# Attention slots joined in pairs on every engine of a two-layer transformer kernel

## The chip, the cores and the metric

The kernel runs on one core of one Trainium2 chip. The metric is the device time of one execution in microseconds. The core has TensorE (PE; its weight loads are shown as PEld), VectorE (DVE), ScalarE (ACT), GpSimd (POOL) and SyncE (SP, which here issues DMAs). Each runs its own instructions in the order in which they are written; they meet at semaphores.

## The reference

x is [8, 512, 256] in float32 (8 batch entries, 512 tokens, width 256). Four layers follow each other, each on the normalized x and added to x: a gated mixer over a context, a feed-forward layer, cross-attention, and a feed-forward layer with 8 experts. The change touches only the cross-attention, which is (cut to what matters):

```python
def _L1_xattn_ref(query, key, value, ...):        # query: layernorm(x); key, value: context
    q = (query @ W_Query + B_Query).reshape(B, Lq, 16, 64)
    k = (key @ W_Key + B_Key).reshape(B, Lk, 16, 64)
    v = (value @ W_Value + B_Value).reshape(B, Lk, 16, 64)
    scores = jnp.einsum('bqhd,bkhd->bhqk', q, k) / D ** 0.5
    probs = jax.nn.softmax(scores, axis=-1)
    out = jnp.einsum('bhqk,bkhd->bqhd', probs, v)
    return out.reshape(B, Lq, 1024) @ W_Output + B_Output
```

## The kernel before

`attention` works on 64 units, one after the other: a unit u is one pair of heads (2 x 64 = 128 rows) of one batch entry, `U = HP * B` with 8 pairs and 8 entries. In a unit there are `NBL` = 8 tiles j: 2 heads by 4 blocks of 128 queries. A tile has 128 x 512 scores. Its way is:

- TensorE, `score` (L905): two matmuls into one of two banks of PSUM (`S_BANK + j % 2`). The operands are of type fp32r. Keys and queries are split into a high and a low part for that. `score` may write a bank when the exponential of tile j - 2 has read it (semaphore `exp`).
- VectorE, `row_max` (L1040): the negated maximum of each row.
- ScalarE (L997): the exponential into one of four tiles `Pr`, and the row's sum.
- VectorE, `row_sum` (L1045): the reciprocal of the sum. GpSimd (L1018): multiplies the tile by it.
- TensorE, `turn` (L916): four transposes of 128 x 128 into one of two banks (`T_BANK`). VectorE, `keep` (L1052), copies them to `PT`; for tiles 4 and 5 ScalarE does it (L1010).

Once per unit there is more. `project` (L884) makes the queries (k = 0) and keys (k = 1) of unit u + 1, `project_values` (L893) its values, `weigh_values` (L926) multiplies the turned tiles of unit u - 1 with its values, and `output` (L936) applies the output weights in two halves, which VectorE's `add_out` (L1059) adds to x. The queries and keys of u + 1 are split: ScalarE's `queries` (L966) and `keys` (L973) write the high part, VectorE's `queries` (L1027) and `keys` (L1034) the low part. The keys are then copied by four DMAs from `k_own` to `k2`, which holds each head's keys twice (L867); SyncE issues them when both parts of the keys are there:

```python
                for u in range(U):
                    sp.wait_ge(s["kh"], u + 1)
                    sp.wait_ge(s["kl"], u + 1)
```

and the first score of the unit waits for their landing:

```python
                    if j == 0:
                        pe.wait_ge(s["ql"], u + 1)
                        pe.wait_ge(s["k2"], 64 * (u + 1))
```

The order is written out by hand on each engine, as a loop over u (65 turns, since the end of a unit's work falls into the next) and over the slots j = 0 to 7. TensorE's slot is `score(u, j)`, then `turn(u, j - 2)`, then the extra work: a projection of unit u + 1 in slots 0 and 1, the weighing of u - 1 in slot 2, the values of u + 1 in slot 4, the outputs of u - 1 in slots 5 and 6. VectorE's slot is `row_sum(u, j - 1)`, `row_max(u, j)`, `keep(u, j - 2)`; its `queries` come in slot 1, its `keys` in slot 2, `add_out` in slot 7. ScalarE's slot is one exponential, with `queries` in slot 0, `keys` in slot 1, `heads_out` (L983, the weighed values of u - 1) in slot 4 and `values` (L978) in slot 5.

Of the kernel before, what the change touches and what calls it, by code (L numbers as in the profile page):

```python
# [17 lines left out]
ACT = mybir.ActivationFunctionType  # L18
# [3 lines left out]
P = 128  # L22
B, S, D = 8, 512, 256
N = B * S
TPB = S // P
# [327 lines left out]
def wait_count(eng, sem, value):  # L353

    if value > 0:
        eng.wait_ge(sem, value)
# [457 lines left out]
def attention(nc, c, x_all, xnT_all, ctxT_all, first, Wq, Wk, Wv, Wo):  # L814
# [3 lines left out]
    with ExitStack() as ctx:  # L818
# [28 lines left out]
        def there(u):  # L847
            return 0 <= u < U
# [6 lines left out]
        with nc.Block() as block:  # L855
# [15 lines left out]
            def _(pe):  # L871
# [37 lines left out]
                def turn(u, j):  # L909
                    pe.wait_ge(s["pn"], NBL * u + j + 1)  # L910
                    if j >= 2:
                        wait_turned_copies(pe, u, j - 1)
                    elif u:
                        wait_turned_copies(pe, u - 1, NBL - 1 + j)
                    for t in range(TPB):
                        ins = pe.transpose(ps[:, T_BANK + j % 2, P * t:P * t + P], Pr[:, j % 4, P * t:P * t + P],  # L916
                                           c["ident"][:, :])
                    ins.then_inc(s["t_ps"], 1)
# [22 lines left out]
                project(0, 1)  # L941
                project_values(0)
                for u in range(U + 1):
                    for j in range(NBL):
                        if there(u):
                            score(u, j)
                            if j >= 2:
                                turn(u, j - 2)
                        if j < 2 and there(u - 1):
                            turn(u - 1, NBL - 2 + j)  # L950
                        if j < 2 and there(u + 1):
                            project(u + 1, j)
                        if j == 2 and there(u - 1):
                            weigh_values(u - 1)
                        if j == 4 and there(u + 1):
                            project_values(u + 1)
                        if j in (5, 6) and there(u - 1):
                            output(u - 1, j - 5)

            @block.scalar  # L960
            def _(act):
                def queries(u):
                    act.wait_ge(s["q_ps"], u + 1)
                    for h in range(2):
                        own = slice(AD * h, AD * h + AD)
                        ins = act.activation(q2[own, u % 2, h, :], ps[own, A_BANK, :], ACT.Identity,  # L966
                                             bias=b_s[own, 0, u % HP:u % HP + 1])
                    ins.then_inc(s["qh"], 1)

                def keys(u):  # L970
                    act.wait_ge(s["k_ps"], u + 1)
                    wait_count(act, s["k2"], 64 * u)
                    act.activation(k_own[:, 0, :], ps[:, A_BANK + 1, :], ACT.Identity,  # L973
                                   bias=b_s[:, 1, u % HP:u % HP + 1]).then_inc(s["kh"], 1)

                def values(u):
                    act.wait_ge(s["v_ps"], u + 1)
                    act.copy(V[:, u % 2, :, :], ps[:, A_BANK, :].rearrange("p (t d) -> p t d", t=TPB)  # L978
                             ).then_inc(s["V"], 1)

                def heads_out(u):
                    act.wait_ge(s["pv"], u + 1)
                    act.activation(oT[:, :], ps[:, O_BANK, :], ACT.Identity, bias=b_s[:, 2, u % HP:u % HP + 1]  # L983
                                   ).then_inc(s["oT"], 1)

                act.wait_ge(s["scaled"], 1)
                queries(0)
                keys(0)
                values(0)
                for u in range(U + 1):  # L990
                    for j in range(NBL):
                        if j == 4 and there(u - 1):
                            heads_out(u - 1)
                        if there(u):
                            act.wait_ge(s["nmax"], NBL * u + j + 1)
                            wait_count(act, s["t_ps"], NBL * u + j - 3)
                            act.activation(Pr[:, j % 4, :], ps[:, S_BANK + j % 2, :], ACT.Exp,  # L997
                                           bias=nmax[:, j % 4:j % 4 + 1], accum_out=rsum[:, j % 4:j % 4 + 1]
                                           ).then_inc(s["exp"], 1)
                        if there(u + 1):  # L1000
                            if j == 0:
                                queries(u + 1)
                            if j == 1:
                                keys(u + 1)
                            if j == 5:
                                values(u + 1)
                        if there(u) and j - 2 in ON_ACT:
                            act.wait_ge(s["t_ps"], NBL * u + j - 1)
                            q = P * ((j - 2) % TPB)
                            act.copy(PT[:, u % 2, (j - 2) // TPB, :, q:q + P],  # L1010
                                     ps[:, T_BANK + j % 2, :].rearrange("p (t q) -> p t q", t=TPB)
                                     ).then_inc(s["pt_a"], 1)

            @block.gpsimd
            def _(pool):
# [6 lines left out]
            def _(dve):  # L1022
# [20 lines left out]
                def row_sum(u, j):  # L1043
                    dve.wait_ge(s["exp"], NBL * u + j + 1)
                    dve.reciprocal(rinv[:, j % 4:j % 4 + 1], rsum[:, j % 4:j % 4 + 1]).then_inc(s["rinv"], 1)  # L1045
# [9 lines left out]
                def add_out(u, half):  # L1055
# [12 lines left out]
                dve.wait_ge(s["w"], 16 * 3)  # L1068
                dve.tensor_scalar(w_rest[:, 0, :, :], w_rest[:, 0, :, :], AD ** -0.5, None, ALU.mult
                                  ).then_inc(s["scaled"], 1)  # L1070
                for u in range(U + 1):
                    for j in range(NBL):
                        if there(u):
                            if j >= 1:
                                row_sum(u, j - 1)
                            row_max(u, j)
                            if j >= 2:
                                keep(u, j - 2)
                        if j < 2 and there(u - 1):
                            keep(u - 1, NBL - 2 + j)  # L1080
                        if there(u + 1):
                            if j == 1:
                                queries(u + 1)
                            if j == 2:
                                keys(u + 1)
                        if j == 7:
                            if there(u):
                                row_sum(u, j)
                            if there(u - 1):
                                if u > 1:  # L1090
                                    dve.wait_ge(s["x"], 2 * (u - 1))
                                add_out(u - 1, 0)
                                add_out(u - 1, 1)


def load_expert_weights(sp, ew, w1, w2):
# [643 lines left out]
```

## Time and profile before

| | |
|---|---|
| Time, median of 3 runs | 1924.83 us (1918.81 to 1925.09) |
| Profiled execution, its own time | 1923.95 us |
| Its span, first to last instruction | 1922.2 us |
| Mean granted clock of TensorE, share of full | 0.925 |
| Busy: TensorE, weight loads, VectorE, ScalarE, GpSimd | 1711.2, 1162.7, 1205.1, 844.4, 645.5 us |
| First and last start of a score (L905) | 471.2 and 1630.3 us |
| Scores' matmuls, transposes (counts) | 1024 and 2048 |
| DMAs of the keys (L867) | 256 of 256 KB |

The profile is that of one execution. Times in it count from the first instruction. TensorE's matmuls overlap and their ends are modelled, so the starts of neighbouring instructions tell the pace, not the durations. "Idle before" is how long an engine stood still before an instruction, and what ended that. The attention stage is the longest stage of the program and lies between 471 and 1645 us.

### The profile page before, as it was taken

Reading aid. Unit: us, or ns where it says so; the run is one execution under the profiler, and the core shown is the slowest. Engines: PE = TensorE matmul, PEld = TensorE weight load, DVE = VectorE, ACT = ScalarE, POOL = GpSimd, SP = SyncE. Lnnn points to the kernel's source line nnn. Section 1 sums busy time; section 2 is a strip of 40 time slices with the busy share of each in tenths; the row PEclk is TensorE's granted clock in tenths of the full one; section 3 lists DMA queues with packets and bytes.
Section 4 is the critical chain, followed back from the end, with each engine's and each line's share of the span. In section 5 each row is a group of like instructions: output and inputs, shape, how many; then the busy total and the mean of one; then the engine's idle time right before and its main releaser. Section 6 shows DMA issues by size and latency. Waiting matters only on the chain. (4 is left out here: it accounts for less than half of the span.)

```text
span 1922.2 us, 26211 instructions
## 1 busy us (share of the span) xinstructions
PE 1711.2 (89%) x8900; PEld 1162.7 (60%) x8900; DVE 1205.1 (63%) x2743; ACT 844.4 (44%) x1870; POOL 645.5 (34%) x745
## 2 busy tenths in 40 slices
PE   6569999996999999999999999999999999742564
PEld 4456777764666666666666666666666666631343
DVE  5444444432777777777777777777777776657731
ACT  3224433332555555555555555555555555110111
POOL 2154444430333323323323333333333233100885
PEclk9669999998999999999999999999999999555777
DMA  7100000003221222222322222212212221250244
GB/s 249 20 22 12 12 12 1 1 0 102 66 66 45 67 64 46 66 59 52 67 53 58 67 49 62 67 44 67 66 45 66 62 49 45 92 176 0 48 73 58
DMA packets 66658, 109.47 MB, mean 57 GB/s; under 512 B 16088, under 2 KB 48096, under 8 KB 66528
## 3 DMA queue, kind: packets, MB, share of 16 engines
q1 hardware_dynamic: 60384, 99.29, 20.9%
q0 software_dynamic: 6144, 8.52, 2.9%
q8 instruction: 72, 1.18, 0.3%
q14 instruction: 58, 0.48, 0.1%
HBM read 27.84 MB, written 12.85 MB: 21 GB/s over the span
## 5 line engine op out<-in xcount | busy, mean ns | idle before, releaser
L1018 POOL TENSOR_SCALAR at_Pr<-at_Pr,at_rinv 128x512 f32<-128x512 f32 x512 | 355.8, 695 | 824.3 <-DVE at_rinv L1045 824.3
L997 ACT ACTIVATE at_Pr<-at_ps,at_nmax 128x512 f32<-128x512 f32 x512 | 352.0, 687 | 522.4 <-DVE at_nmax L1040 520.8
L1040 DVE TENSOR_REDUCE at_nmax<-at_ps 128x1 f32<-128x512 f32 x512 | 351.1, 686 | 138.2 <-PE at_ps L905 127.3
L905 PE MATMUL at_ps<-at_k,at_q 128*128 128x512 f32 x1024 | 420.6, 492 | 9.4 <-DMA at_k<-at_k_own 7.7
L916 PE MATMUL at_ps<-k_ident,at_Pr 128*128 128x128 f32 x2048 | 310.7, 274 | 4.4 <-POOL at_Pr L1018 4.4
L916 PEld LDWEIGHTS at_ps<-k_ident,at_Pr 128*128 128x128 f32 x2048 | 249.3, 140 | 94.1 <-POOL at_Pr L1018 33.2
L1052 DVE COPY at_PT<-at_ps 128x512 f32<-128x512 f32 x384 | 261.5, 681 | 0.0
L905 PEld LDWEIGHTS at_ps<-at_k,at_q 128*128 128x128 f32 x1024 | 174.4, 190 | 129.0 <-issue 119.5
L926 PE MATMUL at_ps<-at_PT,at_V 128*64 128x512 f32 x1024 | 235.5, 602 | 0.9 <-DVE at_PT L1052 0.9
L1045 DVE RECIPROCAL at_rinv<-at_rsum 128x1 f32<-128x1 f32 x512 | 83.4, 163 | 174.9 <-ACT at_Pr L997 173.0
L926 PEld LDWEIGHTS at_ps<-at_PT,at_V 128*64 128x64 f32 x1024 | 68.2, 137 | 122.6 <-issue 121.5
L936 PE MATMUL at_ps<-at_wo,at_oT 128*128 128x256 f32 x512 | 131.6, 380 | 0.8 <-ACT at_oT L983 0.8
L446 PE MATMUL mm_ps<-mx_w,mm_hT 128*128 128x256 f32 x512 | 120.9, 382 | 0.0
L436 PE MATMUL mm_ps<-m_xnT,mx_w 128*128 128x512 f32 x256 | 111.2, 592 | 1.3 <-ACT m_xnT L589 1.3
L893 PE MATMUL at_ps<-at_w_rest,m_ctxT 128*128 128x128 f32 x896 | 109.2, 275 | 0.0
L884 PE MATMUL at_ps<-m_xnT,at_w_rest 128*128 128x512 f32 x224 | 106.8, 599 | 0.0
L884 PE MATMUL at_ps<-m_ctxT,at_w_rest 128*128 128x512 f32 x224 | 105.4, 593 | 0.0
L893 PEld LDWEIGHTS at_ps<-at_w_rest,m_ctxT 128*128 128x128 f32 x896 | 104.5, 192 | 0.0
L446 PEld LDWEIGHTS mm_ps<-mx_w,mm_hT 128*128 128x128 f32 x512 | 93.7, 190 | 16.6 <-issue 5.3
L1027 DVE SCALAR_TENSOR_TENSOR at_q<-at_ps,m_b_all,at_q 64x512 fp32r<-64x512 f32 x128 | 96.0, 750 | 8.3 <-ACT at_q L966 5.4
L997 ACT ACTIVATION_READ_ACCUMULATOR at_Pr<-at_ps,at_nmax 128x1 f32 x512 | 98.6, 193 | 0.0
L936 PEld LDWEIGHTS at_ps<-at_wo,at_oT 128*128 128x128 f32 x512 | 87.4, 190 | 8.3 <-ACT at_oT L983 1.7
(251 smaller groups left out, 2099.1 us busy)
## 6 DMA issues: line engine op xcount, KB each, us to landing
at_k<-at_k_own SPq DMA_DIRECT2D x256, 256.0 KB, 4.2
k_x<-in_x SPq DMA_DIRECT2D x8, 512.0 KB, 7.8
mg_ctx<-in_ctx SPq DMA_DIRECT2D x8, 512.0 KB, 7.9
mx_ctxn<-in_ctx SPq DMA_DIRECT2D x8, 512.0 KB, 3.8
rows<-lo_xn SPq DMA_DIRECT2D x8, 512.0 KB, 3.0
r_w<-in_L_ffn_w SPq DMA_DIRECT2D x16, 256.0 KB, 5.3
out<-k_x SPq DMA_DIRECT2D x1, 4096.0 KB, 16.9
mx_w<-in_L_ffn_w SPq DMA_DIRECT2D x2, 1024.0 KB, 10.3
```

Source lines behind the costliest of these rows:

```text
L436: ins = pe.matmul(ps[:, H_BANK + f % 4, :], w1_s[:, k, P * f:P * f + P], xnT_all[:, k, b * S:b * S + S], start=k == 0, stop=k == DC - 1)
L446: ins = pe.matmul(ps[:, Y_BANK + t // 2, D * (t % 2):D * (t % 2) + D], hT[:, f, P * t:P * t + P], w2_s[:, f, :], start=f == 0, stop=f == F ...
L884: ins = pe.matmul(ps[:, A_BANK + k, :], weights(k, d, hp), src[:, d, b * S:b * S + S], start=d == 0, stop=d == DC - 1)
L893: ins = pe.matmul(ps[:, A_BANK, P * t:P * t + P], ctxT_all[:, d, b * S + P * t:b * S + P * t + P], weights(2, d, hp), start=d == 0, stop=d ...
L905: ins = pe.matmul(ps[:, S_BANK + j % 2, :], q2[:, u % 2, h, q:q + P], k2[:, u % 2, h, part, :], start=part == 0, stop=part == 1)
L916: ins = pe.transpose(ps[:, T_BANK + j % 2, P * t:P * t + P], Pr[:, j % 4, P * t:P * t + P], c["ident"][:, :])
L926: ins = pe.matmul(ps[AD * h:AD * h + AD, O_BANK, :], V[:, u % 2, t, AD * h:AD * h + AD], PT[:, u % 2, h, t, :], start=t == 0, stop=t == TP ...
L936: ins = pe.matmul(ps[:, Y_BANK - half, D * (t % 2):D * (t % 2) + D], oT[:, P * t:P * t + P], wo_s[:, u % HP, :], start=True, stop=True)
L997: act.activation(Pr[:, j % 4, :], ps[:, S_BANK + j % 2, :], ACT.Exp, bias=nmax[:, j % 4:j % 4 + 1], accum_out=rsum[:, j % 4:j % 4 + 1]).th ...
L1018: pool.tensor_scalar(Pr[:, n % 4, :], Pr[:, n % 4, :], rinv[:, n % 4:n % 4 + 1], 1.0, ALU.mult, ALU.mult).then_inc(s["pn"], 1)
L1040: dve.tensor_reduce(nmax[:, j % 4:j % 4 + 1], ps[:, S_BANK + j % 2, :], AX.X, ALU.max, negate=True).then_inc(s["nmax"], 1)
L1052: dve.tensor_copy(PT[:, u % 2, j // TPB, :, q:q + P], ps[:, T_BANK + j % 2, :].rearrange("p (t q) -> p t q", t=TPB)).then_inc(s["pt_v"], 1)
```

## The change

The slots are joined in pairs on TensorE, ScalarE and VectorE. GpSimd and SyncE are as they were. On TensorE a pair slot is two scores, then the eight transposes of the two tiles before, then the extra work of both slots: both projections in slot 0, the weighing in slot 2, the values in slot 4, both outputs in slot 6. On ScalarE a pair slot is two exponentials; `queries` and `keys` of u + 1 both come behind the pair of slot 2, `values` and the copies of tiles 4 and 5 behind the pair of slot 6. On VectorE a pair slot is two maxima, then copy, reciprocal, copy, reciprocal; `queries` come at the end of slot 2, `keys` in slot 4 behind the maxima, and `add_out` one unit later, at the end of slot 0.

```diff
@@ TensorE
                 for u in range(U + 1):
-                    for j in range(NBL):
+                    for j in range(0, NBL, 2):
                         if there(u):
                             score(u, j)
-                            if j >= 2:
+                            score(u, j + 1)
+                            if j:
                                 turn(u, j - 2)
-                        if j < 2 and there(u - 1):
-                            turn(u - 1, NBL - 2 + j)
-                        if j < 2 and there(u + 1):
-                            project(u + 1, j)
+                                turn(u, j - 1)
+                        if j == 0:
+                            if there(u - 1):
+                                turn(u - 1, NBL - 2)
+                                turn(u - 1, NBL - 1)
+                            if there(u + 1):
+                                project(u + 1, 0)
+                                project(u + 1, 1)
                         if j == 2 and there(u - 1):
                             weigh_values(u - 1)
                         if j == 4 and there(u + 1):
                             project_values(u + 1)
-                        if j in (5, 6) and there(u - 1):
-                            output(u - 1, j - 5)
+                        if j == 6 and there(u - 1):
+                            output(u - 1, 0)
+                            output(u - 1, 1)
@@ ScalarE
                 for u in range(U + 1):
-                    for j in range(NBL):
+                    for j in range(0, NBL, 2):
                         if j == 4 and there(u - 1):
                             heads_out(u - 1)
                         if there(u):
...
+                            exponential(u, j)
+                            exponential(u, j + 1)
                         if there(u + 1):
-                            if j == 0:
+                            if j == 2:
                                 queries(u + 1)
-                            if j == 1:
                                 keys(u + 1)
-                            if j == 5:
+                            if j == 6:
                                 values(u + 1)
...
+                        if there(u) and j == 6:
+                            for n in ON_ACT:
+                                keep(u, n)
@@ VectorE
-                for u in range(U + 1):
-                    for j in range(NBL):
+                for u in range(U + 2):
+                    for j in range(0, NBL, 2):
+                        before = (u, j - 2) if j else (u - 1, NBL - 2)
                         if there(u):
-                            if j >= 1:
-                                row_sum(u, j - 1)
                             row_max(u, j)
-                            if j >= 2:
-                                keep(u, j - 2)
-                        if j < 2 and there(u - 1):
-                            keep(u - 1, NBL - 2 + j)
-                        if there(u + 1):
-                            if j == 1:
-                                queries(u + 1)
-                            if j == 2:
-                                keys(u + 1)
-                        if j == 7:
-                            if there(u):
-                                row_sum(u, j)
-                            if there(u - 1):
-                                if u > 1:
-                                    dve.wait_ge(s["x"], 2 * (u - 1))
-                                add_out(u - 1, 0)
-                                add_out(u - 1, 1)
+                            row_max(u, j + 1)
+                        if j == 4 and there(u + 1):
+                            keys(u + 1)
+                        if there(before[0]):
+                            keep(*before)
+                        if there(u):
+                            row_sum(u, j)
+                        if there(before[0]):
+                            keep(before[0], before[1] + 1)
+                        if there(u):
+                            row_sum(u, j + 1)
+                        if j == 0 and there(u - 2):
+                            add_out(u - 2, 0)
+                            add_out(u - 2, 1)
+                        if j == 2 and there(u + 1):
+                            queries(u + 1)
```

How the instructions stand now is shown at three places. In these rows a line number is that of the kernel that is shown (in the changed kernel VectorE's lines are L1039 for the queries, L1046 for the keys, L1052 for the maximum, L1057 for the reciprocal, L1064 for the copy and L1071 for `add_out`).

VectorE before, from the first maximum of a unit (slot 0) to the low keys of the next unit (`at_k_own`), which are followed by the reciprocal of tile 2:

```order
L1040 TENSOR_REDUCE at_nmax<-at_ps 128x1 [waits at_s_ps]
L1052 COPY at_PT<-at_ps 128x4x128 [waits at_t_ps]
L1045 RECIPROCAL at_rinv<-at_rsum 128x1 [waits at_exp]
L1040 TENSOR_REDUCE at_nmax<-at_ps 128x1 [waits at_s_ps]
L1052 COPY at_PT<-at_ps 128x4x128 [waits at_t_ps]
L1027 SCALAR_TENSOR_TENSOR at_q<-at_ps,m_b_all,at_q 64x512 [waits at_qh]
L1027 SCALAR_TENSOR_TENSOR at_q<-at_ps,m_b_all,at_q 64x512
L1045 RECIPROCAL at_rinv<-at_rsum 128x1 [waits at_exp]
L1040 TENSOR_REDUCE at_nmax<-at_ps 128x1 [waits at_s_ps]
L1052 COPY at_PT<-at_ps 128x4x128 [waits at_t_ps]
L1034 SCALAR_TENSOR_TENSOR at_k_own<-at_ps,m_b_all,at_k_own 128x512 [waits at_kh]
L1045 RECIPROCAL at_rinv<-at_rsum 128x1 [waits at_exp]
```

VectorE in the changed kernel, from the end of slot 0 (the two additions to x) to the low keys:

```order
L1071 TENSOR_TENSOR k_x<-at_ps,k_x 128x512 [waits at_y_ps] x2
L1052 TENSOR_REDUCE at_nmax<-at_ps 128x1 [waits at_s_ps] x2
L1064 COPY at_PT<-at_ps 128x4x128 [waits at_t_ps]
L1057 RECIPROCAL at_rinv<-at_rsum 128x1 [waits at_exp]
L1064 COPY at_PT<-at_ps 128x4x128 [waits at_t_ps]
L1057 RECIPROCAL at_rinv<-at_rsum 128x1 [waits at_exp]
L1039 SCALAR_TENSOR_TENSOR at_q<-at_ps,m_b_all,at_q 64x512 [waits at_qh]
L1039 SCALAR_TENSOR_TENSOR at_q<-at_ps,m_b_all,at_q 64x512
L1052 TENSOR_REDUCE at_nmax<-at_ps 128x1 [waits at_s_ps] x2
L1046 SCALAR_TENSOR_TENSOR at_k_own<-at_ps,m_b_all,at_k_own 128x512 [waits at_kh]
```

The low keys stood behind the maxima of tiles 0, 1 and 2 and one copy of slot 2; they now stand behind the maxima of tiles 0 to 5, all four copies of slots 0 and 2, and the additions to x.

TensorE in the changed kernel, from the last turns of a unit's slot 6 over the outputs to the next unit's slot 0, whose first score is the one that waits for `at_k2`:

```order
L916 MATMUL at_ps<-k_ident,at_Pr 128x128 [waits at_pt_a,at_pt_v,at_pn]
L916 MATMUL at_ps<-k_ident,at_Pr 128x128 x3
L936 MATMUL at_ps<-at_wo,at_oT 128x256 [waits at_oT]
L936 MATMUL at_ps<-at_wo,at_oT 128x256 x3
L905 MATMUL at_ps<-at_k,at_q 128x512 [waits at_k2,at_ql,at_exp]
L905 MATMUL at_ps<-at_k,at_q 128x512
L905 MATMUL at_ps<-at_k,at_q 128x512 [waits at_exp]
L905 MATMUL at_ps<-at_k,at_q 128x512
L916 MATMUL at_ps<-k_ident,at_Pr 128x128 [waits at_pt_a,at_pt_v,at_pn]
L916 MATMUL at_ps<-k_ident,at_Pr 128x128 x3
L916 MATMUL at_ps<-k_ident,at_Pr 128x128 [waits at_pt_a,at_pt_v,at_pn]
L916 MATMUL at_ps<-k_ident,at_Pr 128x128 x3
```

Before, one turn of four transposes stood between any two scores, and each projection behind its own score; now both scores, the turns of tiles 6 and 7 of the unit before and both projections stand in this order behind that wait.

## Rows read from the trace of the kernel before

**Rows 1.** The page, busy time, share of the span and instructions of each engine.

```profile
PE 1711.2 (89%) x8900; PEld 1162.7 (60%) x8900; DVE 1205.1 (63%) x2743; ACT 844.4 (44%) x1870; POOL 645.5 (34%) x745
```

**Rows 2.** Stretches: length, busy PE, PEld, DVE, ACT, POOL, then clock, DMA share, GB/s.

```profile
529.10:1601.20 1072.10, 1072.10 (x5666) 706.96 (x5665) 790.98 (x1595) 594.42 (x1359) 328.31 (x473) 1.00 0.26 59
...
1615.00:1631.00 16.00, 13.61 (x69) 8.08 (x69) 10.25 (x23) 7.35 (x19) 4.87 (x8) 1.00 0.00 1
...
1646.00:1652.00 6.00, 0.37 (x3) 0.30 (x4) 5.32 (x24) 0.00 (x0) 2.19 (x2) 0.50 0.01 1
```

**Rows 3.** Timeline, one unit, TensorE's loads (PEld), then its matmuls: start us, us, what.

```profile
706.02 0.30 PEld L905 LDWEIGHTS at_ps<-at_k,at_q 128*128 128x128 f32 x2
...
708.09 0.19 PEld L884 LDWEIGHTS at_ps<-m_xnT,at_w_rest 128*128 128x128 f32 x1 [0.24 <-issue]
708.51 0.19 PEld L905 LDWEIGHTS at_ps<-at_k,at_q 128*128 128x128 f32 x1 [0.24 <-issue]
...
724.18 0.30 PEld L905 LDWEIGHTS at_ps<-at_k,at_q 128*128 128x128 f32 x2
...
712.03 0.60 PE L916 MATMUL at_ps<-k_ident,at_Pr 128*128 128x128 f32 x4
...
716.71 0.60 PE L916 MATMUL at_ps<-k_ident,at_Pr 128*128 128x128 f32 x4
...
717.62 0.60 PE L916 MATMUL at_ps<-k_ident,at_Pr 128*128 128x128 f32 x4
718.05 1.95 PE L893 MATMUL at_ps<-at_w_rest,m_ctxT 128*128 128x128 f32 x16
...
720.31 0.60 PE L916 MATMUL at_ps<-k_ident,at_Pr 128*128 128x128 f32 x4
...
722.08 0.60 PE L916 MATMUL at_ps<-k_ident,at_Pr 128*128 128x128 f32 x4
```

**Rows 4.** Timeline, VectorE: queries, maximum, low keys, maximum.

```profile
711.62 1.51 DVE L1027 SCALAR_TENSOR_TENSOR at_q<-at_ps,m_b_all,at_q 64x512 fp32r<-64x512 f32 x2
...
713.36 0.69 DVE L1040 TENSOR_REDUCE at_nmax<-at_ps 128x1 f32<-128x512 f32 x1
...
714.57 0.74 DVE L1034 SCALAR_TENSOR_TENSOR at_k_own<-at_ps,m_b_all,at_k_own 128x512 fp32r<-128x512 f32 x1
...
716.91 0.69 DVE L1040 TENSOR_REDUCE at_nmax<-at_ps 128x1 f32<-128x512 f32 x1 [1.53 <-PE at_ps L905]
```

**Rows 5.** Timeline, SyncE: issue of the four copies.

```profile
715.38 3.16 SPq L867 DMA_DIRECT2D at_k<-at_k_own  x4
```

**Rows 6.** Line L867, the one issue after 717.2: the last of the four copies.

```profile
DMA to landing us min/median/max: 5.0/5.0/5.0
```

**Rows 7.** Timelines: ScalarE's exponential, VectorE's reciprocal, GpSimd's multiplication.

```profile
711.50 0.69 ACT L997 ACTIVATE at_Pr<-at_ps,at_nmax 128x512 f32<-128x512 f32 x1
712.09 0.19 ACT L997 ACTIVATION_READ_ACCUMULATOR at_Pr<-at_ps,at_nmax 128x1 f32 x1
...
707.43 0.16 DVE L1045 RECIPROCAL at_rinv<-at_rsum 128x1 f32<-128x1 f32 x1 [0.84 <-ACT at_Pr L997]
...
707.76 0.69 POOL L1018 TENSOR_SCALAR at_Pr<-at_Pr,at_rinv 128x512 f32<-128x512 f32 x1 [1.08 <-DVE at_rinv L1045]
```

**Rows 8.** Timeline, TensorE: the first score of the first unit.

```profile
471.21 0.50 PEld L905 LDWEIGHTS at_ps<-at_k,at_q 128*128 128x128 f32 x2 [7.86 <-issue]
```

**Rows 9.** Timeline, TensorE: the first score of the second unit.

```profile
487.70 0.30 PEld L905 LDWEIGHTS at_ps<-at_k,at_q 128*128 128x128 f32 x2
```

**Rows 10.** Line L867, the four copies of one unit, 1042.4 to 1044.2.

```profile
DMA to landing us min/median/max: 2.9/4.3/6.0
```

**Rows 11.** Timeline, TensorE, just behind the stage.

```profile
1645.89 0.38 PE L1197 MATMUL lo_ps<-k_ident,lo_gw 8*128 8x8 f32 x2 [2.60 <-DMA lo_gw<-in_L_ffn_gate_w]
```

**Rows 12.** Timeline, TensorE, weights of the last weighing.

```profile
1637.46 0.24 PEld L926 LDWEIGHTS at_ps<-at_PT,at_V 128*64 128x64 f32 x2 [0.61 <-issue]
1638.31 0.24 PEld L926 LDWEIGHTS at_ps<-at_PT,at_V 128*64 128x64 f32 x2 [0.61 <-issue]
```

More of the change, by code:

```diff
@@ L989, in _, with exponential, keep @@
                 values(0)
+                def exponential(u, j):
+                    act.wait_ge(s["nmax"], NBL * u + j + 1)
+                    wait_count(act, s["t_ps"], NBL * u + j - 3)
+                    act.activation(Pr[:, j % 4, :], ps[:, S_BANK + j % 2, :], ACT.Exp,
+                                   bias=nmax[:, j % 4:j % 4 + 1], accum_out=rsum[:, j % 4:j % 4 + 1]
+                                   ).then_inc(s["exp"], 1)
+                def keep(u, j):
+                    act.wait_ge(s["t_ps"], NBL * u + j + 1)
+                    q = P * (j % TPB)
+                    act.copy(PT[:, u % 2, j // TPB, :, q:q + P],
+                             ps[:, T_BANK + j % 2, :].rearrange("p (t q) -> p t q", t=TPB)).then_inc(s["pt_a"], 1)
                 for u in range(U + 1):
-                    for j in range(NBL):
+                    for j in range(0, NBL, 2):
                         if j == 4 and there(u - 1):
@@ L994, in _ @@
                         if there(u):
[L995 to L999, printed above, removed]
+                            exponential(u, j)
+                            exponential(u, j + 1)
                         if there(u + 1):
-                            if j == 0:
+                            if j == 2:
                                 queries(u + 1)
-                            if j == 1:
                                 keys(u + 1)
-                            if j == 5:
+                            if j == 6:
                                 values(u + 1)
[L1007 to L1012, printed above, removed]
+                        if there(u) and j == 6:
+                            for n in ON_ACT:
+                                keep(u, n)
             @block.gpsimd
```

## The prediction

> **What bounds the kernel now.** I read the page first: TensorE is busy 89% of the span, twice as long as ScalarE and GpSimd, half as long again as VectorE [rows 1]. Then the table of stretches: from 529.1 to 1601.2 us, 56% of the span, TensorE shows no idle time and a clock of 1.00, 2.4 GHz [rows 2]. That is the attention stage, and only this stage changes. Then one unit (one pair of heads, one batch entry) on TensorE, in order of time. The weights of its first score load at 706.02, those of the next unit's at 724.18: a period of 18.16 us [rows 3]. I take the pieces of that period from the starts of neighbouring groups, since the ends are modelled. Four transposes take 0.43 (717.62 to 718.05). The turns at 716.71 and 717.62 have one score between them, so a score with its turn takes 0.91, and a score alone 0.48. A projection is four matmul records at 0.43 each (weights at 708.09 and 708.51): 1.72. From the turn at 712.03 to the turn at 716.71 are 4.68, less 0.43 and 0.48: 3.77 for the weighing of values. The value projection runs from 718.05 to 720.31 less one score, 1.78. One output is 720.31 to 722.08 less 0.91: 0.86 [rows 3]. The unit's sum is 8 x 0.91 + 2 x 1.72 + 3.77 + 1.78 + 2 x 0.86 = 17.99. So TensorE bounds the stage, and all its waits together are 0.17 us per unit.
>
> The second thing to read is a chain with slack: the split keys of the next unit. VectorE makes their low part (L1034) from 714.57 on, in 0.74, so to 715.31 [rows 4]. SyncE then issues four copies from 715.38 on [rows 5]; the last of these starts at 717.2 and lands 5.0 later [rows 6], at 722.2. The first score of the next unit waits for all four. Before the change it comes at 724.18: slack 1.98. Everything below hangs on these two microseconds.
>
> **The change part by part.** No instruction is added or removed; only the order differs.
>
> *TensorE's pairs.* A pair slot is two scores and eight transposes, 2 x 0.91 = 1.82, and then the extra work. Slot 0 has two projections: 5.26. Slot 2 has the weighing: 5.59. Slot 4 has the value projection: 3.60. Slot 6 has two outputs: 3.54. Pairing can save at most the 0.17 of waits, and possibly something where a score follows a score, which no row shows. I take 0; the ends are 0 and, if the second score of a pair needed only the 0.43 that one record of a projection takes for as many columns, 4 x 0.05 per unit. TensorE's own pace is in any case not what ends the unit, as follows.
>
> *The pair's own chain.* Counted from the start of a pair: a maximum starts 0.20 after the turn that follows its score (716.91 against 716.71 [rows 3, 4]), so the first at 0.68, the second 0.61 later. A first exponential starts near 1.4 and takes 0.78 with the reading of its sum [rows 7]: the second ends near 2.97. In VectorE's new order (two maxima, copy, reciprocal, copy, reciprocal) the last reciprocal ends near 3.75. GpSimd starts 0.17 later and takes 0.69 [rows 7]: the second tile can be turned at about 4.7. It is wanted at the slot's length plus 2 x 0.48 and 0.43, so at 4.93 in the shortest slot. The keys add 0.6 to this chain in slot 4: 5.3 against 5.0 wanted. That wait of 0.3 stands ahead of the longer one below and vanishes in it. Nothing else in this chain binds.
>
> *The low keys.* They stood on VectorE behind the third maximum and a copy, and now stand behind the sixth maximum. With the unit's first score as zero, slot 4 starts at 5.26 + 5.59 = 10.85. The fifth maximum starts 0.68 later, at 11.53. Maximum, copy and keys follow each other within 1.21 (713.36 to 714.57 [rows 4]), and a second maximum takes the copy's place, so the keys start at 12.74 and end, after 0.74, at 13.48. Does anything else hold them up? ScalarE's high keys are done at about 10.2: the exponentials of pair 2 end near 8.2, two halves of the queries and the keys follow at the exponential's 0.69 each [rows 7]. VectorE's queries take 1.5 [rows 4] behind the ones of ScalarE and end near 11.1. So neither does. Before, the keys ended at 715.31 and the unit's first score was at 706.13, its weights' start and one transpose's 0.11: 9.18. They come 4.30 later.
>
> *The copies.* From the end of the keys to the last landing is 722.2 less 715.31, 6.9. The landing is at 13.48 + 6.9 = 20.38. To clear the wait and load the first weights I allow 0.2. The next unit's first score starts at **20.57**. TensorE ran out of work at 18.0 and stands for **2.6 us in each unit**. Behind the waiting score are queued the turns of tiles 6 and 7, the projections, everything. The period grows from 18.16 to 20.57, by 2.41.
>
> *The sum.* 62 full periods x 2.41 = 149. In the first unit the same chain is led by the queries: ScalarE ends them after pair 2, and VectorE's part of 1.5 blocks its maxima. I work out about 21 where 16.5 were (471.21 [rows 8] to 487.70 [rows 9]): +4, ends 2 and 6. The last unit has no next keys and gains from overlap: -3, ends 0 and -6. Landings later than usual: in one unit the last took 6.0 instead of 5.0 [rows 10], which the slack swallowed and which now enters the period: +6 in all, ends 0 and 15. The clock, below: +8, ends 0 and 107. Together +164. The profiled execution took 1923.95 for a span of 1922.2, 0.9 under the median of 1924.83. 1923.95 + 164 = **2088**.
>
> *The clock.* An idle stretch of 2.6 us in every unit is new. Just behind the stage an idle time of 2.60 [rows 11] is followed by a clock of 0.50, 1.2 GHz, in the stretch from 1646 on; in the last unit, where TensorE idles 2.4 of 16 us in short pieces, the clock stays 1.00, 2.4 GHz [rows 2]. At half the clock the weighing's pairs start 0.85 apart [rows 12] instead of 0.43; four such pairs are 1.7 lost. So a unit costs either nothing or 1.7 more, and that lies ahead of the keys, on the path. In 63 units it is 107. The gap at 1645.89 had thin work before it, this one has dense work on both sides; I take five units of the 63: 8.
>
> *A rule beside the rows.* Rows give 6.9 from the end of the keys to the last of four copies of 256 KB. The Trainium skill, "DMA: Bandwidth & Descriptors", section "Anatomy of one DMA — SWDGE (gpsimd) path", fits a fixed 2.0 us plus the bytes at 436 GB/s. By that, as an estimate, 1 MB would land after 4.4, the period would be near 18.1, and the time near 1920, unchanged. The fit was made on another engine's queue, and the trace does not agree with it here.
>
> **The rivals.**
> *The transfer stays hidden, and the kernel becomes faster.* One copy of the four takes 4.3 in the median [rows 10]. If the set as a whole landed 4.3 after the keys, the score could start at 13.48 + 4.3 + 0.2 = 17.98, just under TensorE's 17.99. Then the waits of 0.17 would be the gain: 64 x 0.17 = 11, time 1913. The point from which it decides is a landing 4.3 after the keys, or keys 2.6 earlier. Against it: the four are issued one after the other, the last 1.8 after the first [rows 5, 6], and takes 5.0 more.
> *The clock falls in every unit.* +107 instead of +8: time 2187. For it: the 2.60 above. Against it: the dense work on both sides.
> *The pair chain binds too.* If it were 2.5 longer than I count, 7.2 instead of 4.7, the turns in slots 2 and 4 would wait about 0.5 each, ahead of the keys: 63 x 1.0 = 63 more, time 2151. Against it: each of its links is a row.
>
> **How the numbers follow.** Chances: forecast 0.79, clock in every unit 0.12, pair chain 0.04, hidden transfer 0.05. Within the forecast, the sum from slot 0 to the keys may be off by 0.3, 19 us in all; first and last unit 5; landings 0 to 15; clock from 0 to a third of the units, 36. Taken together, not all at their ends at once, that gives about 2060 to 2135; the range is 2058 to 2138 and leaves out most of the second and the last case. About 0.5% (10 us) is what a measurement of this kernel can tell from no change. Faster by more: 0.03, the larger part of the hidden transfer; within it: 0.02; slower: 0.95.
>
> **What would show it.** In the profile of the changed kernel: a wait of the score (L905) for the DMA into the keys in nearly every unit, 2.5 each, some 150 together; a period of about 20.6; the low keys starting 12.7 after the unit's first score; the last copy landing 6.9 after the keys. If the period is near 20.6 but the keys start elsewhere, the sum is right by luck. If TensorE shows no wait for the DMA, the forecast is wrong at its core. Stretches of clock 0.50 inside the stage would say how much the clock adds.

## The result and the profile after

The changed kernel takes 2102.27 us in the median of 4 runs (2091.03 to 2104.61), the kernel before 1923.19 in the 4 runs beside it: a ratio of 1.0915, 95% interval [1.0896, 1.0935]. The profiled execution took 2104.61 with a span of 2102.9. All further times are in us. Kernels marked "one execution" below ran once, so that their time carries no interval; their mean clocks (0.906 to 0.929) are far from the 0.728 of a slow execution of the kernel before (2313), which is left out.

The page of the changed kernel, part 1, answers to [rows 1]. TensorE's busy time (with modelled ends) grew by 28 only, some 17 of it from the lower clock that is read below, and its share of the span fell by six points:

```profile
PE 1739.1 (83%) x8900; PEld 1182.4 (56%) x8900; DVE 1173.7 (56%) x2743; ACT 830.0 (39%) x1870; POOL 637.6 (30%) x745
```

The view of the waits of the changed kernel, from 529 to 1760. A row reads: who waited, for whom, in total, how often, the longest:

```profile
PE at_ps L905 <- DMA at_k<-at_k_own: 142.0, 59, 3.5
...
PEld at_ps L916 <- POOL at_Pr L1030: 4.9, 16, 0.4
```

Before, the wait of the first row came up once in the program, in the first unit (7.7). Now it stands in every unit, 2.4 on average (by the modelled ends of the matmuls before it). The second row is the turn that waits for GpSimd's tile; before it was 24.1 in 59 times from 529.1 to 1601.2.

One unit of the changed kernel on TensorE, in order of time. It answers to [rows 3]:

```profile
708.59 1.17 PE L905 MATMUL at_ps<-at_k,at_q 128*128 128x512 f32 x4 [2.05 <-DMA at_k<-at_k_own]
709.60 1.04 PE L916 MATMUL at_ps<-k_ident,at_Pr 128*128 128x128 f32 x8
710.48 1.88 PE L884 MATMUL at_ps<-m_xnT,at_w_rest 128*128 128x512 f32 x4
...
719.40 1.21 PE L905 MATMUL at_ps<-at_k,at_q 128*128 128x512 f32 x4
720.45 1.04 PE L916 MATMUL at_ps<-k_ident,at_Pr 128*128 128x128 f32 x8
721.32 1.95 PE L893 MATMUL at_ps<-at_w_rest,m_ctxT 128*128 128x128 f32 x16
...
724.99 1.89 PE L936 MATMUL at_ps<-at_wo,at_oT 128*128 128x256 f32 x8
729.25 0.47 PE L905 MATMUL at_ps<-at_k,at_q 128*128 128x512 f32 x1 [2.36 <-DMA at_k<-at_k_own]
```

The four matmuls of two scores in a row, then eight transposes, then the extra work. Behind the outputs TensorE stands still, 2.36 by its modelled ends, and what ends that is the DMA into the keys. The same unit on VectorE and SyncE answers to [rows 4, 5]:

```profile
720.18 1.29 DVE L1052 TENSOR_REDUCE at_nmax<-at_ps 128x1 f32<-128x512 f32 x2 [0.62 <-PE at_ps L905]
721.50 0.75 DVE L1046 SCALAR_TENSOR_TENSOR at_k_own<-at_ps,m_b_all,at_k_own 128x512 fp32r<-128x512 f32 x1
...
722.33 3.14 SPq L867 DMA_DIRECT2D at_k<-at_k_own  x4
```

The view of line L867 for the last two of these four issues, 723.5 and 724.2, answers to [rows 6]:

```profile
DMA to landing us min/median/max: 4.5/4.7/4.9
```

The fifth and sixth maximum, then the low keys until 722.25; the last issue is at 724.2, its landing 4.9 later, at 729.1; the score's weights load at 729.22. Over the stage this chain is nearly the same in each unit. From the starts of the units' first scores in the trace, the median period is 20.64 (18.17 before).

The sum of the difference in span, 180.7, from those starts (before: 471.21, 487.70, 1614.35; after: the three rows below):

```profile
475.46 0.50 PEld L905 LDWEIGHTS at_ps<-at_k,at_q 128*128 128x128 f32 x2 [8.85 <-issue]
...
497.56 0.93 PEld L905 LDWEIGHTS at_ps<-at_k,at_q 128*128 128x128 f32 x3 [4.27 <-issue]
...
1799.66 0.76 PEld L905 LDWEIGHTS at_ps<-at_k,at_q 128*128 128x128 f32 x4 [2.69 <-issue]
```

| Stretch | before | after | difference |
|---|---|---|---|
| up to the first score of the first unit | 471.2 | 475.5 | +4.3 |
| first unit | 16.5 | 22.1 | +5.6 |
| 62 units | 1126.7 | 1302.1 | +175.4 |
| last unit to the end | 307.9 | 303.2 | -4.6 |

The first line is not the change's. The code ahead of the stage is untouched, and other kernels of this study, whose code there is the same too, begin their first score anywhere from 470.2 to 475.5 (one kernel, traced on two occasions, at 471.5 and 474.3). Of the 175.4, 62 x 2.47 = 153 are the longer period. The clock's record has 35 us of clock 0.50 between the second and the last unit; half of that, 17.5, is lost. The last 5 are landings that came later than usual.

### The profile page after: what moved, and what is told of

Same layout as the page of the kernel before. It is cut to its first block and busy times, and to the rows that moved or that the text cites. A ratio compares the mean times of both kernels' runs of the same rounds, so it can differ in the third digit from the quotient of the medians.

```text
span 2102.9 us, 26148 instructions
## 1 busy us (share of the span) xinstructions
PE 1739.1 (83%) x8900; PEld 1182.4 (56%) x8900; DVE 1173.7 (56%) x2743; ACT 830.0 (39%) x1870; POOL 637.6 (30%) x745
## 5 line engine op out<-in xcount | busy, mean ns | idle before, releaser
L1030 POOL TENSOR_SCALAR at_Pr<-at_Pr,at_rinv 128x512 f32<-128x512 f32 x512 | 348.0, 692 | 1009.8 <-DVE at_rinv L1057 1009.6
L999 ACT ACTIVATE at_Pr<-at_ps,at_nmax 128x512 f32<-128x512 f32 x512 | 347.1, 683 | 664.5 <-DVE at_nmax L1052 664.3
L1052 DVE TENSOR_REDUCE at_nmax<-at_ps 128x1 f32<-128x512 f32 x512 | 330.1, 686 | 419.4 <-PE at_ps L905 419.3
L905 PE MATMUL at_ps<-at_k,at_q 128*128 128x512 f32 x1024 | 324.3, 438 | 162.5 <-DMA at_k<-at_k_own 161.8
L916 PE MATMUL at_ps<-k_ident,at_Pr 128*128 128x128 f32 x2048 | 279.3, 278 | 0.8 <-POOL at_Pr L1030 0.6
L916 PEld LDWEIGHTS at_ps<-k_ident,at_Pr 128*128 128x128 f32 x2048 | 241.5, 142 | 47.6 <-POOL at_Pr L1030 8.1
L1064 DVE COPY at_PT<-at_ps 128x512 f32<-128x512 f32 x384 | 257.4, 677 | 1.9 <-PE at_ps L916 1.7
L1039 DVE SCALAR_TENSOR_TENSOR at_q<-at_ps,m_b_all,at_q 64x512 fp32r<-64x512 f32 x128 | 96.0, 750 | 59.7 <-ACT at_q L972 58.7
L936 PE MATMUL at_ps<-at_wo,at_oT 128*128 128x256 f32 x512 | 121.2, 380 | 0.8 <-ACT at_oT L989 0.8
L884 PE MATMUL at_ps<-m_xnT,at_w_rest 128*128 128x512 f32 x224 | 117.0, 649 | 0.0
L1057 DVE RECIPROCAL at_rinv<-at_rsum 128x1 f32<-128x1 f32 x512 | 79.7, 156 | 48.8 <-ACT at_Pr L999 48.8
L936 PEld LDWEIGHTS at_ps<-at_wo,at_oT 128*128 128x128 f32 x512 | 92.3, 190 | 11.6 <-ACT at_oT L989 1.7
```

Source lines behind the costliest of these rows:

```text
L884: ins = pe.matmul(ps[:, A_BANK + k, :], weights(k, d, hp), src[:, d, b * S:b * S + S], start=d == 0, stop=d == DC - 1)
L905: ins = pe.matmul(ps[:, S_BANK + j % 2, :], q2[:, u % 2, h, q:q + P], k2[:, u % 2, h, part, :], start=part == 0, stop=part == 1)
L936: ins = pe.matmul(ps[:, Y_BANK - half, D * (t % 2):D * (t % 2) + D], oT[:, P * t:P * t + P], wo_s[:, u % HP, :], start=True, stop=True)
L1030: pool.tensor_scalar(Pr[:, n % 4, :], Pr[:, n % 4, :], rinv[:, n % 4:n % 4 + 1], 1.0, ALU.mult, ALU.mult).then_inc(s["pn"], 1)
L1052: dve.tensor_reduce(nmax[:, j % 4:j % 4 + 1], ps[:, S_BANK + j % 2, :], AX.X, ALU.max, negate=True).then_inc(s["nmax"], 1)
L1064: dve.tensor_copy(PT[:, u % 2, j // TPB, :, q:q + P], ps[:, T_BANK + j % 2, :].rearrange("p (t q) -> p t q", t=TPB)).then_inc(s["pt_v"], 1)
```

## The experiments

The theory: the low keys stand too late on VectorE, and the copies behind them no longer fit before the next unit. Rivals: the pairing itself costs (bank order, transposes behind transposes), or the clock does. In all kernels below the three other layers are as they were.

**Keys ahead of queries (e1_keys_first).** The changed kernel, with the keys moved forward:

```diff
@@ ScalarE
                             if j == 2:
-                                queries(u + 1)
                                 keys(u + 1)
+                                queries(u + 1)
@@ VectorE
-                        if j == 4 and there(u + 1):
-                            keys(u + 1)
...
                         if j == 2 and there(u + 1):
+                            keys(u + 1)
                             queries(u + 1)
```

> The changed kernel with the next unit's keys ahead of its queries, both behind the pair of slot 2 on ScalarE and VectorE (keys leave slot 4). Theory, the low keys come too late for the copies: they now end near 9.9 us after the unit's first score, the last copy lands near 16.9, TensorE is out of work at 18.0; the wait is hidden, the period falls from 20.6 to 18.0 and the time to 1912 to 1920. Rival, the pairing itself costs the time (banks, order of scores and transposes): the period stays above 19.5, the time above 2030. Rival, the clock is the larger part: with the wait gone it goes too, so this run alone cannot tell it from the theory.

Measured: 1906.46 (1906.16 to 1909.39), ratio to the kernel before 0.9904 [0.9888, 0.9921]. The wait is gone; the low keys end 9.55 after the unit's first score, and the median period is 17.96. In its trace the score of a unit waits for the copies twice in the whole program, 8.7 in all:

```profile
  DMA at_k<-at_k_own: 8.7, 2
```

Of the 8.7, 8.0 stand ahead of the first unit. So the pairing itself costs nothing: with the keys placed for it the kernel is 1% faster than the one before. The time is 6 below the expected band, though the period is as expected. In the profile the last unit and what follows took 302.4 instead of 307.9; when the same kernel was traced again (e1_again) they took 305.7, so about 3 of that differs from one execution to the next.

**The late keys without pairs (e2_late_keys_unpaired).** The kernel before, one line moved:

```diff
@@ VectorE
-                            if j == 2:
+                            if j == 4:
                                 keys(u + 1)
```

> The kernel before, unpaired, with one edit: VectorE's low keys in slot 4 instead of slot 2. Theory: they end near 14.3 us after the unit's first score instead of 9.2, the copies land 6.9 later, the period becomes about 21.3 us, and the time 1923 + 62 x 3.15 = about 2120, up to 2180 if the clock falls in more units. Rival, the pairing costs the time: this kernel stays within 1% of 1923.

Measured: one execution, 2173.18. The waits of this kernel from 529 to 1800, and its table of stretches (columns as in [rows 2]):

```profile
PE at_ps L905 <- DMA at_k<-at_k_own: 173.9, 57, 3.9
```

```profile
529.00:1800.00 1271.00, 1094.95 (x5492) 714.74 (x5490) 777.91 (x1548) 589.91 (x1320) 317.95 (x460) 0.95 0.22 49
```

One late instruction, without any pairing, makes a kernel slower by 13%. The mean clock of 0.95 in the stage says that part of it is the clock: its record has 31 low stretches inside the stage, 123 long in all, so about 61 lost, a quarter of the 248. Without them the mean period would be 22.18 - 61 / 62 = 21.2, and 21.20 is the median of the units without a low stretch; 21.3 was worked out.

**The keys ahead of the maxima (e3_keys_before_maxima).** The changed kernel; `keys(u + 1)` stays in slot 4, but stands ahead of the two maxima.

> The changed kernel with the low keys still in slot 4, but ahead of the two maxima. Theory: they start when VectorE's queries end, near 11.1 us after the unit's first score, 1.6 us earlier than now; the period falls by as much, to about 19.0, and the time to about 1975. If the wait were for something else than the keys, the time would not follow their place one for one.

Measured: one execution, 1970.45. In its trace the keys now follow the queries at once:

```profile
712.84 1.51 DVE L1039 SCALAR_TENSOR_TENSOR at_q<-at_ps,m_b_all,at_q 64x512 fp32r<-64x512 f32 x2 [0.86 <-ACT at_q L972]
714.38 0.75 DVE L1046 SCALAR_TENSOR_TENSOR at_k_own<-at_ps,m_b_all,at_k_own 128x512 fp32r<-128x512 f32 x1
```

The keys end 11.66 after the unit's first score against 13.58, 1.92 earlier; the median period is 18.74 against 20.64, 1.90 shorter. The period follows the place of the keys one for one. The score still waits for the copies, 0.6 in the median and 1.7 at most, and from 499 to the last unit's start the clock does not fall.

**Pairs on TensorE alone (e4_pairs_on_pe_only).** TensorE's loop as changed, the loops of ScalarE and VectorE as before (with keys in their slots 1 and 2).

> Pairs on TensorE alone; ScalarE and VectorE keep the order of the kernel before, with the low keys in their slot 2. Theory: no wait for the copies; but each second maximum stands behind the first tile's exponential, so the second tile is ready about 5.1 us after the pair's start against 4.9 wanted in the shortest slot, and ScalarE's queries hold up an exponential in slot 0: period 18.0 to 18.7, time 1915 to 1955. Rival, pairs on TensorE cost the time by themselves: near 2100.

Measured: 1986.02 (1985.24 to 1989.26), ratio 1.0311 [1.0294, 1.0328], period 19.20. Both expectations missed. No unit but the first waits for the copies, so the rival's 2100 is out; but I had priced the singles too low. From its timeline, slot 0 of a unit:

```profile
704.94 1.38 ACT L972 ACTIVATE at_q<-at_ps,m_b_all 64x512 fp32r<-64x512 f32 x2 [0.72 <-PE at_ps L884]
...
706.35 0.69 ACT L1003 ACTIVATE at_Pr<-at_ps,at_nmax 128x512 f32<-128x512 f32 x1
...
707.18 0.30 PEld L905 LDWEIGHTS at_ps<-at_k,at_q 128*128 128x128 f32 x2 [0.53 <-ACT at_Pr L1003]
...
708.98 0.20 PEld L916 LDWEIGHTS at_ps<-k_ident,at_Pr 128*128 128x128 f32 x2 [0.87 <-POOL at_Pr L1024]
```

ScalarE's queries stand ahead of the second tile's exponential. TensorE now projects only behind two scores and eight transposes, so ScalarE waits 0.72 for the projection, and the exponential comes at 706.35. TensorE first waits for it with the next pair's second score, then for GpSimd's tile behind it.

**The same, with the queries moved (e9_queries_moved).** In the kernel above:

```diff
@@ ScalarE
-                            if j == 0:
-                                queries(u + 1)
                             if j == 1:
+                                queries(u + 1)
                                 keys(u + 1)
@@ VectorE
-                            if j == 1:
-                                queries(u + 1)
                             if j == 2:
                                 keys(u + 1)
+                            if j == 3:
+                                queries(u + 1)
```

> Pairs on TensorE alone, as in the run that took 1986 us, but with the once-per-unit work placed for them: ScalarE's queries and keys both behind the exponential of slot 1, VectorE's keys in slot 2 and its queries in slot 3. Theory: that run lost 1.2 us per unit because ScalarE's queries waited for TensorE's projection ahead of the second exponential of slot 0; with them behind it the period falls from 19.2 to 18.0 to 18.2 us and the time to 1908 to 1925. Rival, single slots on VectorE (a reciprocal between two maxima) are what cost: the period stays above 18.8, the time above 1955.

Measured: 1911.27 (1905.45 to 1913.87), ratio 0.9921 [0.9898, 0.9944], period 17.97. So the follower engines need not go in pairs. What counts is which once-per-unit instruction stands ahead of which tile's work. This run moved the queries on both engines; which of the two moves gave the 1.23 per unit is not separated.

**The first kernel again (e1_again).** The kernel of the first experiment, unaltered.

> The same kernel as the first run of this study, beside the one above on the same chip: 1904 to 1910 us.

Measured: 1909.26 (1905.1 to 1913.45), ratio 0.9916 [0.9892, 0.994], period 17.96: the same as on the other occasion, and no different from the kernel above.

**Filling the wait (e5_filler).** The changed kernel; nothing in the chain of the keys is altered:

```diff
@@ TensorE, score
                     if j == 0:
+                        if u:
+                            for _ in range(10):
+                                pe.matmul(ps[:, S_BANK, :], q2[:, (u - 1) % 2, 0, 0:P], k2[:, (u - 1) % 2, 0, 0, :],
+                                          start=True, stop=True)
                         pe.wait_ge(s["ql"], u + 1)
```

> The changed kernel with ten more matmuls per unit, of the unit's old keys and queries into the free score bank, placed ahead of TensorE's wait for the copies; they take about 2.3 us, less than the wait. Their result is overwritten. The path from the first score to the keys is untouched. Theory on the clock: the nine stretches of clock 0.50 inside the stage vanish, the period of a unit stays near 20.6 us, and the time falls by 9 x 1.7 to about 2087. Rival, the clock's share is not tied to TensorE's idle time: the stretches stay, and the time stays near 2102 or rises.

Measured: 2088.08 (2086.2 to 2091.15), ratio to the kernel before 1.0848 [1.0824, 1.0871], against 1.0915 [1.0896, 1.0935] for the changed kernel. The median period is still 20.64, and the idle time ahead of a unit's first score fell from 2.35 to 0.04 in the median. The clock's record has no low stretch from 473 to 1801 (the first unit starts at 470, the last at 1782); from 529 to 1760 (columns as in [rows 2]):

```profile
529.00:1760.00 1231.00, 1217.65 (x6266) 828.63 (x6265) 760.77 (x1594) 582.98 (x1360) 321.57 (x474) 1.00 0.23 52
```

More work on TensorE, less time. In the two profiled executions it takes 1311.4 instead of 1324.2 from the first unit's first score to the last unit's: some 18 less for the low clock, and 6 more of late landings, which differ from one execution to the next. How a low stretch looks in the changed kernel, in its table of stretches and on TensorE behind the wait:

```profile
731.00:734.00 3.00, 3.00 (x7) 1.49 (x6) 2.78 (x7) 1.15 (x4) 1.36 (x2) 0.50 0.00 0
734.50:739.50 5.00, 5.00 (x25) 2.77 (x25) 2.60 (x6) 1.87 (x5) 0.48 (x1) 1.00 0.00 0
```

```profile
732.35 0.33 PEld L884 LDWEIGHTS at_ps<-m_xnT,at_w_rest 128*128 128x128 f32 x1 [0.52 <-issue]
733.20 0.33 PEld L884 LDWEIGHTS at_ps<-m_xnT,at_w_rest 128*128 128x128 f32 x1 [0.52 <-issue]
```

The wait ends at 729.2, the clock then falls to 0.50 (1.2 GHz) from 730.7 to 734.1 while TensorE is busy, and the projection's records go at 0.85 instead of 0.43.

**Filling the wait of the unpaired kernel (e8_late_keys_filled).** The kernel of the second experiment with fourteen such filling matmuls in the same place.

> The unpaired kernel with its low keys in slot 4 (2173 us, 31 stretches of low clock inside the stage, 123 us long) with fourteen such filling matmuls ahead of the wait. Theory on the clock: no stretch of low clock is left in the stage, the period is 21.2 in every unit, the time 2173 less half of 123, about 2112. Rival: the stretches stay, the time is 2173 or more.

Measured: one execution, 2124.21 against 2173.18. No low stretch is left from 481 to 1836 (the first unit starts at 475, the last at 1817), and the median period is 21.21. It is 12 above the 2112 expected: 4 of that lie ahead of the stage (its first score is at 475.5 against 471.9), 1 in the first unit and 4 in more late landings (mean period 21.32). The last 3 or so stay open; half of the low stretches may be a little more than they cost.

**Half the bytes behind the low keys (e6_split_copies).** The changed kernel; SyncE copies the high part as soon as it is made (the counts that the others wait for on `k2` are doubled with it):

```diff
@@ SyncE
-                    sp.wait_ge(s["kh"], u + 1)
-                    sp.wait_ge(s["kl"], u + 1)
-                    for h in range(2):
-                        for half in range(2):
-                            sp.dma_start(k2[AD * half:AD * half + AD, u % 2, h, :, :].bitcast(F32),
-                                         k_own[AD * h:AD * h + AD, :, :].bitcast(F32)).then_inc(s["k2"], 16)
+                    for part, made in enumerate(("kh", "kl")):
+                        sp.wait_ge(s[made], u + 1)
+                        for h in range(2):
+                            for half in range(2):
+                                sp.dma_start(k2[AD * half:AD * half + AD, u % 2, h, part, :].bitcast(F32),
+                                             k_own[AD * h:AD * h + AD, part, :].bitcast(F32)).then_inc(s["k2"], 16)
```

> The changed kernel with the copies of the keys' high part issued as soon as ScalarE has made it, so that only four copies of 128 KB are left behind the low part. Theory, the path is low keys, issue, transfer, landing: from the keys' end to the last landing it takes 4.8 to 5.5 us instead of 6.9, the period is 18.6 to 19.3, the time 1965 to 2010. Rival, the landing is bound by something that does not depend on the bytes: it stays near 6.9 and the time near 2100.

Measured: one execution, 1928.13. The theory's direction holds and the rival is out, but the number expected was far off: from the keys' end to the last landing it takes 4.16 in the median instead of 6.85, and the period is 18.06. Line L867 of this kernel:

```profile
DMA to landing us min/median/max: 2.2/2.4/5.5
```

A copy of half the size lands 2.4 after its issue in the median, against 4.5 in the changed kernel. This one edit takes back nearly all of the 9%, with the low keys as late as in the changed kernel. The landing still ends the unit: the first score's weights load 0.1 behind it in the median, and 13.7 to the keys' end, 4.16 and 0.2 are the period. TensorE runs out of work at nearly the same time.

## Why the prediction was right

Forecast 2088 with a range of 2058 to 2138, slower with 0.95; measured 2102.27. Point by point:

- **TensorE's slots.** Slot 4's first score was expected 10.85 after the unit's first; in the unit shown it is 10.84. TensorE had no more work at 17.95, forecast 18.00 (the last output's weights load at 726.29, those before it 0.22 apart; the unit's first at 708.56). So it stands 2.7 in each unit, forecast 2.6. A score behind a score takes 0.466 instead of the 0.48 taken: the small gain that I had left at 0 exists.
- **The low keys.** Start 12.74 forecast, 12.83 measured; end 13.48 against 13.58. The tenth comes from the place behind a maximum: the keys follow the maximum by 0.71, where they followed a copy by 0.60.
- **The copies.** 6.9 forecast, 6.85 in the median. The two things beside it hold as well. The weights load 0.1 after the landing, which with the 0.11 from the weights to the score is the 0.2 allowed. The wait of the turn for the tile behind the keys, expected at 0.3, is there and hidden: among slot 6's eight transposes the weights of the fifth follow those of the fourth by 0.25 instead of 0.11, so it waits 0.15.
- **The period.** 20.57 forecast, 20.64 measured. 62 x 2.41 = 149 became 62 x 2.47 = 153.
- **The clock.** The term that was sized too low: 8 forecast, about 17 measured. I took five low stretches of the 63; nine lie wholly in the units after the second, and one more, longer, at the passage from the first unit to the second. The price of one, 1.7, was right: 20.6 became 22.3 in those units, and the low keys ended that much later. Which units it would strike was not forecast and stays open: most waits of the same length were not followed by a fall. The runs of this kernel spread over 13.6 us, 2091 to 2105, those of the filled kernel over 5. That fits a number of falls that differs from run to run, but does not show it: only one execution was traced, and e1_again, whose trace has no low stretch from its second unit's start to its last's, spread over 8.
- **The ends.** First unit +4 forecast, +5.6 measured, with low clock at both its ends; last unit -3 and -4.6, within the 3 by which that end differed between two traces of one kernel. Late landings +6 and about +5. The rest of what the span lies above the forecast is the 4.3 ahead of the stage, which no term of the sum could hold. So the time is 14 above 2088 for the clock first, then for the period and for that stretch.
- **The rivals.** The pair chain did not bind. Its price was also worked out too high: by its own terms, 7.2 against the 6.65 wanted in slot 2 is a wait of 0.55, and slot 4's turn, wanted at 6.98 and put off by that wait, would not wait, so some 35 and not 63. The hidden transfer did not happen, since the copies land as late after the keys as before. But the point from which it was to decide, keys 2.6 earlier, fits: 1.9 earlier (the third experiment) leaves a period of 18.74, 4.0 earlier (the first) one of 17.96, and the straight line through the first two places reaches 17.96 at 2.7. With the keys 4.0 earlier the rival comes true: faster by 1%, where 1913 had been worked out and 1906 was measured.
- **The rule beside the rows.** By the fixed cost and rate cited from the Trainium skill, "DMA: Bandwidth & Descriptors", section "Anatomy of one DMA — SWDGE (gpsimd) path", applied to the whole set, the kernel would have stayed near 1920 (an estimate). The copies took 6.85 after the keys against its 4.4, so for this queue and this set of four the trace does not agree. But the page gives the fit for a single DMA, and its estimate for one copy is 2.3 for 128 KB and 2.6 for 256 KB. The copies of 128 KB landed 2.2 to 2.4 after their issue (medians of a set's four), which agrees, though it is another queue; of those of 256 KB the first of a set took 3.0 and the last 4.9, which does not. The prediction's use of it also left out that the four are issued one after the other, 1.8 from the first to the last.
- **The two sizes.** With half the bytes the set took 4.16 instead of 6.85. A straight line through the two gives 194 GB/s and 1.5 without any bytes. That 1.5 is not a fixed cost: the issues alone lie 1.8 apart from first to last at both sizes.

## What to carry to other kernels

Before reordering a bounding engine, list the chains that today end with slack, above all those with a DMA, and redo each one's sum in the new order: here 2 us of slack were spent by moving one instruction of 0.74 us to a place 4.4 us later in the unit. When instructions are grouped, the once-per-unit work must be placed anew, by what waits for its result and by what stands behind it. An idle stretch that comes back in every period can cost more than its length, since the clock may fall with it.

## What the runs showed of the hardware

- Idle stretches of TensorE of about 2.4 us, with dense work on both sides, were followed by a low clock in 9 of some 60 units, and most of the others were just as long. With waits of 3.1 us on average (the unpaired kernel with late keys) there were 31 low stretches; with waits of 0.6 us in the median, 1.7 at most (the keys ahead of the maxima), none from 499 to the last unit's start. With ten or fourteen useless matmuls in the gap there was none either (from 473 and 481 on), and the time went down by 14 and 49.
- Four copies of 256 KB between partitions of SBUF, issued over 1.8 us, land 6.85 after their source is ready; four of 128 KB 4.16. In the first case each takes longer than the one before (3.0, 4.0, 4.6 and 4.9 from issue to landing, medians in the changed kernel), as if they queued behind each other; in the second they land as they are issued, every 0.6 to 0.7, each 2.2 to 2.4 after its issue (medians).
